# First edge layer of a two-layer graph network: group sums in a PSUM bank of their own and earlier in the step, and one wide matmul in place of two narrow ones

## The reference

```python
h = gelu(edge_attr_8 @ Wfc1 / sqrt(8))        # 8 -> 64, per edge
h = gelu(h @ Wfc2 / sqrt(64))                 # 64 -> 64
w = h @ Wfc3 / sqrt(64)                       # 64 -> 192, split into w0 64, w1 64, w2 32, w3 32
gs, gv = f_s[src], f_v[src]                   # node rows of the edge's source
mid0 = w0 * gs * y0                           # y0, y1: the four numbers of edge_attr_4
mid1 = w3 * einsum('euc,ec->eu', gv, y1) / sqrt(3)
mid2 = (w1 * gs)[:, :, None] * y1[:, None, :]
mid3 = w2[:, :, None] * gv * y0[:, None, None]
mid_s, mid_v = segment_sum over dst of (mid0, mid1), (mid2, mid3)
x = layernorm(x + sc + alpha(mid_s) * (mid @ Wl2))
```

## Time and profile before

| what | value |
|---|---|
| median of 3 runs | 2632.79 us (2631.97 to 2643.34) |
| profiled execution: its span, first to last instruction | 3060.6 us |
| profiled execution: own time beside its span | none is recorded; the span stands for it |
| its mean granted TensorE clock | 0.813 |
| busy: PE, PEld, DVE, ACT, POOL | 86%, 65%, 54%, 32%, 66% |

### The profile page before, as it was taken

The page is one execution under the profiler, slowest core; times in us unless marked ns, Lnnn a source line. Parts: engine busy times, 40 slices in busy tenths (PEclk is TensorE's granted clock), DMA queues, the critical chain, the costliest instruction groups (busy, mean ns, idle before and its releaser), DMA issues.

```text
span 3060.6 us, 78767 instructions
## 1 busy us (share of the span) xinstructions
PE 2639.6 (86%) x24556; PEld 1983.6 (65%) x24556; DVE 1645.1 (54%) x4537; ACT 984.7 (32%) x2591; POOL 2008.3 (66%) x1630
## 2 busy tenths in 40 slices
PE   7667777886768877876799999999999999999997
PEld 4334444443434444443588888888888888888883
DVE  3446434443444444444466666666666666666664
ACT  2212212221221221221244444444444444444442
POOL 4555554555555555555188888888888888888885
PEclk5566656657676566566699999999999999999998
DMA  6233332332233233332388888888888888888877
GB/s 193 59 96 93 86 89 77 89 93 79 82 93 83 81 95 82 86 94 80 83 140 141 141 141 140 141 141 139 141 141 140 140 140 142 140 140 140 141 136 176
DMA packets 392755, 356.11 MB, mean 116 GB/s; under 512 B 60112, under 2 KB 343440, under 8 KB 392368
## 3 DMA queue, kind: packets, MB, share of 16 engines
q0 software_dynamic: 150528, 141.40, 32.0%
q1 hardware_dynamic: 237552, 208.10, 24.3%
q10 hardware_dynamic: 4544, 4.93, 0.5%
HBM read 246.44 MB, written 133.44 MB: 124 GB/s over the span
## 4 chain that ended last, share of the span: by engine, by line
PE 77%; issue 9%; another core or an unknown queue 8%; DVE 2%; ACT 2%; DMA 1%; POOL 1%; SPq 0%; ACTq 0%; DVEq 0%; POOLq 0%
PE ps_o L1051 11%; PE ps_w L1039 10%; PE ps_d L1060 8%; PE ps_o L1049 8%; PE ps_w L901 7%; PE ps_pg L842 6%; PE ps_x L1073 6%; PE ps_h L894 6%; PE ps_h L888 3%; PE ps_x L1013 3%; PE ps_pg L857 2%; PE ps_pg L851 1%; PE ps_pg L854 1%; PE ps_nd L917 1%
## 5 line engine op out<-in xcount | busy, mean ns | idle before, releaser
L623 POOL DMA_INDIRECT tab<-summed,sidx x784 | 1223.2, 1560 | 284.4 <-issue 230.8
L605 POOL DMA_INDIRECT gat<-f,gidx x784 | 753.4, 961 | 694.7 <-DVE feats L1358 384.9
L1498 DVE TENSOR_TENSOR prod<-ps_w,xg 128x768 f32<-128x768 f32 x392 | 375.4, 958 | 266.3 <-PE ps_w L1039 252.7
L1051 PE MATMUL ps_o<-ro_v,prod 128*128 128x96 f32 x3136 | 479.1, 275 | 0.0
L842 PE MATMUL ps_pg<-feats,sel 128*32 128x320 f32 x1568 | 225.9, 661 | 265.7 <-issue 265.5
L1051 PEld LDWEIGHTS ps_o<-ro_v,prod 128*128 128x128 f32 x3136 | 414.1, 192 | 0.0
L797 ACT ACTIVATE xg<-ps_x 128x768 f32<-128x768 f32 x392 | 296.4, 808 | 341.3 <-PE ps_x L1073 340.3
L1039 PE MATMUL ps_w<-hid,wf 64*128 64x128 f32 x4704 | 368.7, 289 | 2.0 <-ACT hid L798 2.0
L1049 PE MATMUL ps_o<-ro_s,prod 96*128 96x96 f32 x1568 | 327.5, 291 | 19.0 <-DVE msg L1509 4.8
L1039 PEld LDWEIGHTS ps_w<-hid,wf 64*128 64x128 f32 x4704 | 293.5, 187 | 70.2 <-issue 44.6
L1060 PE MATMUL ps_d<-msg,same 128*128 128x193 f32 x1568 | 332.3, 334 | 0.7 <-ACT summed L816 0.7
(11 more groups left out here) (262 smaller groups left out, 3451.0 us busy)
## 6 DMA issues: line engine op xcount, KB each, us to landing
xt<-in_src_rows SPq DMA_DIRECT2D x196, 256.0 KB
xt<-feat SPq DMA_DIRECT2D x784, 36.0 KB
xt<-in_ea SPq DMA_DIRECT2D x196, 128.0 KB
feat<-xt SPq DMA_DIRECT2D x25, 576.0 KB
hot_dst<-in_dst_rows SPq DMA_DIRECT2D x98, 128.0 KB
gat<-f,gidx POOLq DMA_INDIRECT x784
hot_dir<-sh_rows SPq DMA_DIRECT2D x98, 128.0 KB
xt<-hot_dst SPq DMA_DIRECT2D x196, 64.0 KB
```

The lines of the kernel that those rows point to most:

```text
L605: pool.indirect_dma_start(out=gat[:, r % 4, k, :], out_offset=None, in_=t["f0"], in_offset=bass.IndirectOffsetOnAxis(ap=gidx[:, r // 4, at ...
L623: pool.indirect_dma_start(out=t["tabs"][into[k]], out_offset=bass.IndirectOffsetOnAxis(ap=sidx[:, r, k:k + 1], axis=0), in_=summed[:, r, k ...
L1051: last = pe.matmul(ps_o[:, k, 96 + 64 * c:192 + 64 * c], prod[:, ur % 2, k, 1 + c, :], ro_v[:, c, :], start=True, stop=True)
L1498: dve.tensor_tensor(prod[:, r % 2, :, :, :].rearrange("p k c e -> p k (c e)"), ps_w4[:, :, 0:3 * P], xg[:, r // 2, r % 2 * 2:r % 2 * 2 + 2 ...
```

## The change

In the first layer, and with it in the data's layout:

- `layer1` is one matmul of 256 columns on 16 partitions into `ps_h`; the bank `ps_hy` is gone, the first gelu is one instruction of 256 columns, `ea8` is 16 rows of 256 instead of 48 rows of 128, and the weights `w1` are loaded once.
- The freed bank, `ps_sum`, holds both group sums `ps_g`. `tile_sums` no longer waits for `acc_done`.
- PE issues `window_sums(s-3)` between `layer2(s)` and `layer3(s-1)` instead of behind `layer3`.
- DVE does `add_window(s-2)` between `select(s)` and `products(s)` instead of behind `products`.

Nothing else moves: gathers, ACT's order, SP's order and the second layer stay.

```diff
-            w1 = sb(c2, "w1", [48, P])
+            w1 = sb(c2, "w1", [16, P])
-            ea8 = sb(c2, "ea8", [48, 2, P])
+            ea8 = sb(c2, "ea8", [16, 2, 256])
...
-            ps_hy = pb(c2, "ps_hy", [P, 512])
-            ps_h1 = [ps_h[:, 0:P], ps_hy[:, 0:P]]
+            ps_sum = pb(c2, "ps_sum", [P, 512])
+            ps_h1 = ps_h[:, 0:256]
...
-            ps_g = [ps_pg[:, FEAT + 4 * WIN * i:FEAT + 4 * WIN * (i + 1)] for i in range(2)]
+            ps_g = [ps_sum[:, 4 * WIN * i:4 * WIN * (i + 1)] for i in range(2)]
...
                 def load_ea8(u, r):
                     since(sp, h1_ready, u - 1)
-                    sp.dma_start(ea8[:, r, :], t["ea8"][:, bass.ds(u * P, P)]).then_inc(ea8_in[r], 16)
+                    sp.dma_start(ea8[:, r, :], t["ea8"][:, bass.ds(u * 256, 256)]).then_inc(ea8_in[r], 16)
...
-                    for q in range(2):
-                        last = act.activation(h1[:, r % 2, P * q:P * q + P], ps_h1[q], ACT.Gelu_apprx_tanh, scale=8.0 ** -0.5)
-                    last.then_inc(g1_done, 1)
+                    act.activation(h1[:, r % 2, :], ps_h1, ACT.Gelu_apprx_tanh, scale=8.0 ** -0.5).then_inc(g1_done, 1)
...
                 def layer1(u, r, j):
                     pe.wait_ge(ea8_in[r], 16 * (j + 1))
                     since(pe, g2_done, u)
-                    for q in range(2):
-                        at = slice(32 * q, 32 * q + 16)
-                        last = pe.matmul(ps_h1[q], w1[at, :], ea8[at, r, :], start=True, stop=True)
-                    last.then_inc(h1_ready, 1)
+                    pe.matmul(ps_h1, w1[:, :], ea8[:, r, :], start=True, stop=True).then_inc(h1_ready, 1)
...
                             since(pe, part_done, u)
-                            since(pe, acc_done, u)
                             pe.wait_ge(sel_ready, u + 1)
                             pe.wait_ge(prod_done, u + 1)
                             tile_sums(pe, ur, part_ready)
                         if runs(s, NGRP):
                             layer2(s, r)
-                        v, _, vr = lagged(s, j, r, 1, 2)
-                        if runs(v, NGRP):
-                            layer3(v, vr)
                         if runs(u, NGRP):
                             pe.wait_ge(part_done, u + 1)
                             pe.wait_ge(place_ready, u + 1)
                             since(pe, acc_done, u)
                             window_sums(pe, parts[:, ur, :], place[:, ur, :, :], ur, agg_done)
+                        v, _, vr = lagged(s, j, r, 1, 2)
+                        if runs(v, NGRP):
+                            layer3(v, vr)
...
                             select(s, r % 2, pad_off[:, bass.ds(s * G, G)], s + 1)
-                            products(s, j, r)
                         u, _, ur = lagged(s, j, r, 2, 4)
                         if runs(u, NGRP):
                             base = dve.value_load(base_i[0:1, bass.ds(u, 1)], min_val=0, max_val=N)
@@
                             add_window(ur % 2, base)
                         if runs(s, NGRP):
+                            products(s, j, r)
                             positions(r % 2, slot_rel[:, bass.ds(s, 1)])
```

More of the change, by code:

```diff
@@ L393, in _ @@
                 for h in range(2):
-                    for q in range(2):
-                        sp.dma_start(w1[32 * q + 8 * h:32 * q + 8 * h + 8, S * h:S * h + S], t["L0_gnn_Wfc1"]).then_inc(w_in, 16)
+                    sp.dma_start(w1[8 * h:8 * h + 8, S * h:S * h + S], t["L0_gnn_Wfc1"]).then_inc(w_in, 16)
                     sp.dma_start(w2[S * h:S * h + S, S * h:S * h + S], t["L0_gnn_Wfc2"]).then_inc(w_in, 16)
@@ L678, in _ @@
                 act.activation(src_f[:, :], src_i[:, :], ACT.Copy).then_inc(src_set, 1)
-                act.wait_ge(w_in, 16 * 8)
+                act.wait_ge(w_in, 16 * 6)
                 act.activation(w3[:, :], w3raw[:, :], ACT.Copy, scale=1.0 / 8.0).then_inc(w3_ok, 1)
@@ L879, in _ @@
                 pe.wait_ge(res_ready, NT)
-                pe.wait_ge(w_in, 16 * 8)
+                pe.wait_ge(w_in, 16 * 6)
                 pe.wait_ge(w3_ok, 1)
@@ L1686 @@
         "ea3": cols(pad(arr["edge_attr_3"], EP, 1)), "ea4": cols(pad(arr["edge_attr_4"], EP, 0)),
-        "ea8": np.zeros((48, NGRP * P), np.float32),
+        "ea8": np.ascontiguousarray(ea8.reshape(NGRP, 2, 2, P, 8).transpose(1, 4, 0, 2, 3)).reshape(16, NGRP * 256),
         "ea64": np.ascontiguousarray(ea64.reshape(NGRP, 2, 2, P, 64).transpose(0, 2, 4, 1, 3)).reshape(NGRP, P, 256),
     }
-    halves = ea8.reshape(NGRP, 2, 2, P, 8).transpose(2, 1, 4, 0, 3).reshape(2, 16, NGRP * P)
-    data["ea8"][0:16], data["ea8"][32:48] = halves[0], halves[1]
     for name in arr:
```

## The result

The changed kernel takes 2734.19 us (median of 4 runs, 2708.28 to 2776.23) against 2632.38 for the kernel before: a ratio of 1.0333, 95% interval 1.0284 to 1.0382. The ratio leaves out the run of 2776.23 us, which is over 1.5% above the fastest and counts as slow; the medians alone would give 1.0387. The kernel is slower by some 88 us (by the ratio) to 102 us (by the medians), and outside the predicted range (2530 to 2650). The profiled execution took 2733.32 us, with a span of 2731.1.

What follows compares the result with a forecast made beforehand. Gathers were taken to bound the first layer, 5.01 us a group before and after. Only 2 to 3 us drop out at its end: 2628 from the profile's sum, 2630 from the median; forecast 2629 us, range 2530 to 2650.

Steps and rivals of the forecast that it cites:

- the pace of before: First layer: gathers, not the PE-DVE loop, set the pace in the runs, 5.01 us a group, 981 us in all.
- The wait ahead of the tile sums: First layer, PE: the wait for the add goes, 1.37 us at the full clock, 0.88 at the lower, without node work.
- PE's cost of a group: First layer after the change, without node work: 5.66 + 0.36 us at the lower clock, 3.15 + 0.23 at the full.
- The wide matmul: First layer's one 256-column matmul: 1.15 us lower, 0.63 full; adds 0.36 or 0.23 us a group.
- The copy's cover: PE, first layer: the second layer's 0.63 us hides the tile-sum copy before the group sums; at most 0.1 us a group.
- the likeliest case: First layer: gathers set the pace before and after; 2618 to 2643 us, chance 0.51.
- Group sums ahead of the third layer: PE's new order in the first layer: costs nothing, at most 0.1 us a group if the copy is late.
- Adds ahead of the products: DVE's new order in the first layer: products may wait behind a late add, but their waiters have slack; nothing.
- the rival of the falling clock: First layer: longer PE waits bring the lower clock to over 43% of groups; 2698 us at 55%, chance 0.12.
- The sign of being wrong that the prediction named last: First layer: the prediction is wrong if the lower clock covers most groups.
- The inference from the traced execution: First layer: the profiled execution's extra 429 us are the PE-DVE loop at the lower clock and late signals, absent from runs.

Runs made afterwards that it cites:

- second trace: The kernel before, unchanged, traced again for an execution as long as its runs: 2645.95 us, span 2644.0, granted clock 0.83 from 500 to 1000 us.
- e3: Changed kernel with both PE's and DVE's old orders put back, own bank and wide matmul kept: 2621.46 us, ratio 0.9955.
- e6: Changed kernel with PE's old order alone put back (third layer ahead of group sums): 2637.49 us, ratio 1.0018.
- e7: Changed kernel with DVE's old order alone put back (products ahead of the add): 2717.22 us, ratio 1.0342.
- e4: Changed kernel with the wide first-layer matmul over 128 rows, zeros in those beyond 16: 2618.43 us, ratio 0.9951.
- e1: Kernel before with the wide first-layer matmul alone; old bank, wait and orders stay: 2652.06 us, ratio 1.0068.
- e10: e3 with the group sums of the group before, placed between first layer and tile sums: 2640.61 us, ratio 0.9978.
- e12: e3 with the group sums of the group before, placed between second and third layer: 2797.75 us, ratio 1.0586.
- e8: Changed kernel with the wide first-layer matmul over 64 rows, the upper 48 zeros: 2624.57 us, ratio 0.9966.
- e2: Kernel before with the new PE and DVE orders alone; row tiles, shared bank and wait stay: 2682.29 us, ratio 1.0182.
- e11: e3 with the group sums of the group before, placed between tile sums and second layer: 2647.89 us, ratio 1.0006.

## Why the prediction was wrong

**What held.** The gathers do set the pace of before in its runs: the second trace has 5.05 us a group in the middle of the layer, for a forecast of 5.01, and 1018.8 us in all for 981. The wait ahead of the tile sums went. PE's cost of a group was foretold to the hundredth: 5.66 + 0.36 = 6.02 us at the lower clock and 3.15 + 0.23 = 3.38 at the full, and the rows above show 6.02 and 3.38. The wide matmul takes 1.15 us to the next start at the lower clock (566.27 - 565.12) and 0.63 at the full (179.33 - 178.70), as taken from the second layer's row. The copy's cover held too: the group sums follow the second layer 0.63 us after its start at the full clock. Where PE keeps its old order the forecast is even about right in time: 0.9955 for e3, at the lower edge of the likeliest case's own range, 2618 to 2643 us.

**The step that failed** is the one headed *Group sums ahead of the third layer*, priced at "nothing, at most 0.1 us a group". Its cost was some 83 to 102 us by the ratios (e6 against after, e3 against e7, which differ in PE's order alone), and in none of the terms by which I priced it: no wait, no instruction and no cover. I priced an order by what it makes late; here the order changed how long PE stayed at the lower clock, from 11 us at a stretch (e6) to 50 (after). It does so with the first layer on 16 rows; over 128 rows the same order cost nothing (e4). The step *Adds ahead of the products*, priced at nothing as well, cost some 17 us (e6 against e3).

**Behind it stands a second error**, in the rival of the falling clock, which is the case that came and had 0.12. Its arithmetic was right. At 0.67 of granted clock 66% of 500 us are at the lower level, 330 us, which at 6.7 us a group are 49 of the 90 groups that the 361 gathers make up: 55%, by chance the very share that I had picked as an example and for which I gave 2698 us. The sign of being wrong that the prediction named last, the lower clock on most groups, has come. The measured pace there is 5.54 us, not 5.35, because the other groups take 170 / 41 = 4.1 us each instead of 3.7; PE stands idle for 21.8 of the 500 us, which covers that. But the mechanism was another. I had the clock fall more often, by longer waits at the full clock; the full clock lasts about as long in after as in before's second trace (19 and 21 us at a stretch), and it fell less often, 13 times against 29 between 76 and 1000 us. It failed to rise. And my argument against this rival was that at the lower clock PE's work "now has no gaps at all". The rule beside it, from the Trainium skill (TensorE: Matmul & The Clock Gate, section HAM oscillation for the gaps and Part 1 for the release), that idle gaps take the clock down and steady work brings it back, is not borne out in its second half: 98% busy from 195 to 386 us at 0.50, and so the measurement decides.

**The inference from the traced execution** misled in a smaller way. The first trace of before has a clock of 0.63 in the first layer, so 0.67 in after would have read as a gain. The trace that is like the runs has 0.83, and against it after's first layer is longer, not shorter. The releasers "remote" of the earlier trace rows stand in the first trace alone, and no wait of the second names one; that they are late signals stays a guess.

**The wide matmul** was priced at 0.23 to 0.36 us a group, 45 to 71 us where PE sets the pace all through; e1 lost 0.7%, some 18 us; that PE sets the pace only part of the time would explain it, but no run shows that apart. The gain that the bank gives, with the wait that it removes, shows between e1 and e3, which differ in nothing else: 2652.06 to 2621.46, 31 us. The prediction had 2 to 3 us for it, at the layer's end, and the 38 us that before loses to the gathers' pace as given.

**What stays open.** That the sequence of the same matmuls and the rows of the first layer's matmul decide how soon the clock rises is shown, by e6 and e7, by e10 to e12 and by e4 and e8. Which property of the sequence counts is only argued. With a first layer of 16 rows the orders that are fast have two or all three of the dense pieces in a row with the third layer behind the second; after, e2, e7 and e12 have the group sums right ahead of the third layer. A kernel with the thin pieces side by side and the third layer right behind them would tell the length of the dense run from this neighbourhood; it wasn't tried, since the second layer would then stand close ahead of the next group's first layer, with which it shares a bank. Why the first trace of before lasted 3060.6 us is open as well: its stretches at the full clock are 6 us long on the mean, against 21 in the second.

## What to carry to other kernels

Where the granted clock changes within a layer, price a step at both clocks, and the lower first: here a group costs PE 3.38 or 6.02 us against the gathers' 5.01, so an edit that prolongs the stay at the lower clock loses more than any wait it removes. Judge an order of matmuls also by what the granted clock does under it, in rows of a trace that lasts as long as the runs do. And if a small contraction has to stay, zero rows in its operands need cost no time: over 128 rows the first layer takes 0.62 us to the next start at the full clock (e4, 409.32 to 409.94), over 16 rows 0.63.

## What the runs showed of the hardware

- PE can be busy all the time and stay at 1.2 GHz: 98% of 191 us in after. "Keep it busy" is not enough to get the full clock back.
- The same matmuls in another sequence, at 5.85 to 6.02 us a step, change the mean stay at the lower clock from 16 us (e10, e11) to 47 (e12) and the kernel's time by some 6%.
- The first layer over 128 rows instead of 16, the 112 others zeros, brought the mean stay at the lower clock from 50 us to 11, with the order of after unchanged.
